# State-space convolution with LoRA tiles on one core: the first eight heads of the kernel K in two halves, warm-up matmuls from the start, D partly added on VectorE, and the eighth pair of x behind strip 2

## The chip, the cores and the metric

The kernel runs on one core of a Trainium2 chip. Its time is the device time of one execution in microseconds (us). TensorE is the matrix engine (PE in the rows), VectorE is DVE, ScalarE is ACT, GpSimd is POOL, and SyncE (SP) only issues transfers here. Sixteen DMA engines serve all queues. PEld is TensorE loading its stationary operand beside its own matmuls.

## The reference

Two stages over x of shape (128, 32, 512): batch, head, position.

```python
# stage 1: a long convolution by head, K computed from the parameters
dtA = (-exp(log_A_real) + 1j * A_imag) * exp(log_dt)[:, None]
K   = 2 * einsum('hn,hnl->hl', Cc * (exp(dtA) - 1) / A, exp(dtA[:, :, None] * arange(512))).real
y   = causal_conv(x, K) + x * D[:, None]          # by FFT in the reference
x   = x + y * (arange(512) < length[b])
# stage 2: a linear layer of 512 x 512 and a LoRA adapter chosen by batch row
x   = x + x @ W.T + bias + (x @ A[id].T) @ B[id].T
```

## The kernel before

**K.** For each of 32 heads the 512 values of K are a 16 x 32 product over the states, so a head is one small matmul (128x16 by 128x32, both real parts stacked). VectorE makes the factors from sines and magnitudes, which ScalarE computes; POOL and VectorE make the small coefficients (`sm`, `rc`, `mm`, `ct`) ahead of that. The heads go in four groups of eight (`GROUPS`, `group` on VectorE and on TensorE). A group's product in PSUM gets D added at lag 0 by one more small matmul (`row0` by `d_sb`, L915). ScalarE rounds the group to the short form (`k_hi`, L479) and copies it (L482), VectorE subtracts to get the remainder (`k_low`, L670), and ScalarE's queue stores both into a padded array in HBM, `k_pad` (L487).

**Convolution.** For each head, SP loads a "strip" from `k_pad`: 128 partitions, each the same 512 pairs shifted by one position, 512 KB (`load_strip`, L263). TensorE multiplies it with x of that head in twelve matmuls (L932, `head`): four lengths (512, 384, 256 and 128 columns), each for high x high, remainder x high and high x remainder. There are six strip buffers, so strip n is issued once head n - 6 is done. Strip 0 comes in two halves of 256 KB. x arrives in pairs of heads of 512 KB (`load_pair`, L240), eight pairs ahead of everything and the others behind certain strips (`X_AT`). The adapter's A and B and the weight w come in halves behind strips too (`A_AT`, `B_AT`, `W_AT`). ScalarE rounds x (L462), VectorE subtracts (L741) and masks each head's result into `z_all` (L747).

**Tiles.** Behind the convolution 32 tiles of 128 rows follow. `first_tile` and `tile_base` (L981 to L989, L971) multiply by w, `tile_h` (L959) by the gathered A, `tile_b` (L997, L998) adds h times the gathered B. B's table is written to HBM and gathered from there by POOL (L417). The x tiles 0 to 3 (`x_t`), the two table stores and the bias are issued on SP behind strips 30 and 31. On VectorE x tile 2 is added (`x1_of`, L792) ahead of h of tile 0 (`h_masked`, `h_remainder`, L811).

**What sets the order.** Every engine runs its list as written; semaphores hold it where the program says. All loads and strips are on SP's one queue, in the order of the code. Until its first strip TensorE runs 15 and 2 warm-up matmuls (`keep_warm`, L904), whose result isn't used.

Of the kernel before, what the change touches and what calls it, by code (L numbers as in the profile page):

```python
# [6 lines left out]
F32 = mybir.dt.float32  # L7
# [48 lines left out]
GROUPS = ((0, 8), (8, 16), (16, 24), (24, 32))  # L56
G = 8
NG = len(GROUPS)
XS = 4
# [21 lines left out]
K_AFTER = {2: 7, 3: 14}  # L81
WARM_0, WARM_1 = 15, 2
# [7 lines left out]
def build(nc, x_conv, x_tile, params, table, d_row, length, ids_all, w_t, bias, a_t, b_rows, out):  # L90
    ctx = ExitStack()
    with ctx:
# [40 lines left out]
        k_hi = sb("k_hi", [NA, G, NC], F32R)  # L133
        k_sb = sb("k_sb", [NA, KS, G, NC, 2])
# [54 lines left out]
        k_stored, pad_stored, strip_begun = sem("k_stored"), sem("pad_stored"), sem("strip_begun")  # L189
# [7 lines left out]
        k_hi_put = sem("k_hi_put")  # L197
# [40 lines left out]
        def _(sp):  # L238
# [17 lines left out]
            for n in range(2, PRE):  # L256
                load_pair(n)

# [10 lines left out]
            for h in range(NH):  # L269
                for k, (h0, h1) in enumerate(GROUPS):  # L270
                    if h == h0:
                        sp.wait_ge(k_stored, 16 * (k + 1))
                if h >= SS:
                    sp.wait_ge(conv_done, h + 1 - SS)
                if h == 0:
                    load_strip(h, 0, 0, L // 2, strip_begun)
                    load_strip(h, 0, L // 2, L, strip_landed[0])
# [49 lines left out]
        def _(pool):  # L327
            steps = [0]

            def link(ins):  # L330
# [6 lines left out]
            g.memset(zero[:, :], 0.0).then_inc(zeroed, 1)  # L337
            link(g.memset(row0[:, :], 0.0))
            g.memset(row0[:, 0:1], 1.0).then_inc(zeroed, 1)
            link(g.memset(eye[:, :], 0.0))  # L340
            g.affine_select(out=eye[:, :], in_=eye[:, :], compare_op=ALU.not_equal, fill=1.0,
                            base=0, pattern=[[-1, P]], channel_multiplier=1).then_inc(eye_ready, 1)
            pool.wait_ge(eye_ready, 1)
# [9 lines left out]
            link(g.tensor_scalar(par[:, 3:5, :], par[:, 3:5, :], tab[:, NL:NL + 1], None, ALU.mult))  # L353
            link(g.tensor_tensor(sm[:, 1, :], ai, ai, ALU.mult))
            link(g.tensor_tensor(sm[:, 6:8, :], par[:, 4:6, :], twice(ai), ALU.mult))
            pool.wait_ge(ea_ready, 1)
            link(g.tensor_tensor(sm[:, 0, :], ea[:, :], ea[:, :], ALU.mult))
            link(g.tensor_tensor(sm[:, 2, :], sm[:, 0, :], sm[:, 1, :], ALU.add))
            link(g.tensor_scalar(rc[:, 0, :], sm[:, 2, :], 0.5, None, ALU.mult))
            link(g.tensor_tensor(sm[:, 4:6, :], par[:, 2:4, :], twice(ea[:, :]), ALU.mult))  # L360
            link(g.tensor_tensor(mm[:, 0, 0, :], sm[:, 4, :], sm[:, 6, :], ALU.subtract))
            link(g.tensor_tensor(mm[:, 0, 1, :], sm[:, 5, :], sm[:, 7, :], ALU.add))
            pool.wait_ge(th_ready, 1)
# [9 lines left out]
            link(g.tensor_tensor(mm[:, 1, 1, :], sm[:, 6, :], sm[:, 4, :], ALU.subtract))  # L373
            link(g.tensor_tensor(mm[:, 1, 0, :], sm[:, 5, :], sm[:, 7, :], ALU.add))
# [3 lines left out]
            pool.wait_ge(factors, 2)  # L378

            g.iota(pos, pattern=[[P, LC], [0, NB]], base=0, channel_multiplier=1).then_inc(pos_ready, 1)  # L380
# [70 lines left out]
        def _(act):  # L451
# [12 lines left out]
            def group_sines(k):  # L464

                n = GROUPS[k][1] - GROUPS[k][0]
                act.wait_ge(reduced, k + 1)
                act.activation(sines[:, 0:n, :], xx[:, 0:n, :], ACT.Sin, scale=TURN).then_inc(sines_ready, 1)

            def group_store(k):  # L470

                (h0, h1), s = GROUPS[k], k % KS
                n = h1 - h0
                act.wait_ge(k_done, k + 1)
                if k >= KS:
                    act.wait_ge(k_stored, 16 * (k + 1 - KS))
                if k >= 1:
                    act.wait_ge(k_lo_done, k)
                act.activation(k_hi[:, 0:n, :], k_ps[0:NA, s, 0:n * NC].rearrange("a (h c) -> a h c", c=NC),  # L479
                               ACT.Copy).then_inc(k_hi_done, 1)  # L480
                act.wait_ge(k_hi_done, k + 1)
                act.activation(k_sb[:, s, 0:n, :, 0], k_hi[:, 0:n, :].bitcast(F32), ACT.Copy).then_inc(k_hi_put, 1)  # L482
                act.wait_ge(k_hi_put, k + 1)
                act.wait_ge(k_lo_done, k + 1)
                if k >= 1:
                    act.wait_ge(k_stored, 16 * k)
                act.dma_start(k_pad[h0:h1, P:PAD, :].rearrange("h (a c) e -> a h (c e)", a=NA),  # L487
                              k_sb[:, s, 0:n, :, :].rearrange("a h c e -> a h (c e)")
                              ).then_inc(k_stored, 16)
# [6 lines left out]
            act.activation(ea[:, :], par[:, 0, :], ACT.Exp).then_inc(ea_ready, 1)  # L496
            act.wait_ge(zr_ready, 1)
            act.activation(th[:, :], zr[:, :], ACT.Tanh, scale=0.5).then_inc(th_ready, 1)
            act.wait_ge(table_in, 16)
# [18 lines left out]
            magnitudes(18, 24)
            split_x(3)
            for h in range(XS, NH):  # L520
# [89 lines left out]
        def _(dve):  # L610
# [54 lines left out]

            def k_low(k):

                n, s = GROUPS[k][1] - GROUPS[k][0], k % KS
                dve.wait_ge(k_hi_done, k + 1)
                V.tensor_tensor(k_sb[:, s, 0:n, :, 1], k_ps[0:NA, s, 0:n * NC].rearrange("a (h c) -> a h c", c=NC),  # L670
                                k_hi[:, 0:n, :].bitcast(F32), ALU.subtract).then_inc(k_lo_done, 1)

            def group(k):

                (h0, h1), s = GROUPS[k], k % KS
# [4 lines left out]
                def wide(a, m):  # L680
                    return a[:, h0:h1].unsqueeze(2).to_broadcast((P, n, m))

                def turns():
                    link(V.tensor_tensor(u[:, :, NA:NA + NL], wide(turn, NL), lag, ALU.mult))
# [14 lines left out]

                def multiply():  # L700

                    dve.wait_ge(sines_ready, k + 1)
# [3 lines left out]
                    link(V.tensor_tensor(g2[:, 0:n, :, :], sines[:, 0:n, 0:2 * NA].rearrange("p h (o a) -> p h o a", o=2),  # L706
                                         both, ALU.mult))
                    link(V.tensor_tensor(gg[:, s, 0:n, :], g2[:, 0:n, 0, :], g2[:, 0:n, 1, :], ALU.add))

                def scale():  # L710
                    dve.wait_ge(mags, h1)
                    V.tensor_tensor(gg[:, s, 0:n, :], gg[:, s, 0:n, :], mag[:, h0:h1, 0:NA], ALU.mult).then_inc(factors, 1)
                    V.tensor_tensor(ee[:, s, 0:n, :], sines[:, 0:n, 2 * NA:NA + NL], mag[:, h0:h1, NA:NL],
                                    ALU.mult).then_inc(factors, 1)

                return [turns, phases, whole, fraction, multiply, scale]
# [34 lines left out]
            turns, phases, whole, fraction, multiply, scale = group(0)  # L751
# [7 lines left out]
            multiply()  # L759
            scale()  # L760
            turns, phases, whole, fraction, multiply, scale = group(1)
            turns()
            phases()
            whole()
            k_low(0)
            fraction()
            remainder(0)
# [3 lines left out]
            k_low(1)  # L771
# [4 lines left out]
            beside = {h: do for k, at in STEPS_AT.items() for h, do in zip(at, group(k))}  # L776
            for h in range(XS, NH):
                head(h - XS)
                for k, last in K_AFTER.items():
                    if h == last + XS:  # L780
                        k_low(k)
# [117 lines left out]
        def _(pe):  # L899

            def keep_warm(n):

                for _ in range(n):
                    nc.tensor.matmul(y_ps[:, 0, :], xp[:, 0, 0, 0, :], xp[:, 0, :, 0, :], start=True, stop=True)  # L904

            def group(k):
# [5 lines left out]
                for i in range(h1 - h0):  # L912
                    nc.tensor.matmul(k_ps[0:NA, s, i * NC:(i + 1) * NC], gg[:, s, i, :], ee[:, s, i, :],  # L913
                                     start=(i == 0), stop=False)
# [3 lines left out]
            def head(h):  # L918

                if h == 0:  # L920
                    pe.wait_ge(strip_begun, 16)
# [6 lines left out]
                for n, (m, t, e) in enumerate(terms):  # L928

                    if h == 0 and (m, t, e) == (LC // 2, 0, 0):  # L930
                        pe.wait_ge(strip_landed[0], 16)
# [157 lines left out]
```

## Time and profile before

| | us |
|---|---|
| median of 3 runs | 210.45 (210.29 to 210.97) |
| profiled execution | 210.57 |
| its span | 208.5 |

| engine | busy us | share of the span |
|---|---|---|
| TensorE matmul | 190.8 | 91% |
| VectorE | 168.1 | 81% |
| ScalarE | 120.9 | 58% |
| POOL | 90.3 | 43% |

The span runs from the first to the last instruction on the device. A busy share is an average over stages with different limits, so it is the stages that are read: K and preload to about 21 us, convolution to about 86 us, tiles from there. Matmuls are pipelined and the length of one in a row is longer than its step from the one before.

### The profile page before, as it was taken

The page shows a single profiled execution, that of the slowest core. Times are in us where ns is not written, and L with a number is a line of the kernel's source. Part 1 is how long each engine was busy: PE and PEld are TensorE (multiplying, and loading weights), DVE is VectorE, ACT ScalarE, POOL GpSimd, SP SyncE. Part 2 cuts the span into 40 slices and gives each one's busy share as a digit, 9 for nine tenths or more (in the row PEclk, how much of TensorE's full clock was granted, in tenths as well). Part 3 has the DMA queues.
Part 4 walks back from the last instruction along what each step waited for, and adds up shares of the span by engine and source line. Part 5 has one row for each costly group of instructions (what it writes and reads, how often), then busy time and mean ns, then how long its engine had stood idle before and what let it go on. Part 6 is the DMA issues. An engine that isn't in the chain of part 4 may idle for free.

```text
span 208.5 us, 4394 instructions
## 1 busy us (share of the span) xinstructions
PE 190.8 (91%) x1063; PEld 166.4 (80%) x1063; DVE 168.1 (81%) x368; ACT 120.9 (58%) x354; POOL 90.3 (43%) x144
## 2 busy tenths in 40 slices
PE   0049999999999999899999999999999999999994
PEld 0037999999999899787888888888888888888883
DVE  3985598789799976877999978788888878888662
ACT  2798974343736446237767656657566565656530
POOL 4850000001356778085564645546455464545500
PEclk9999999999999999999999999999999999999999
DMA  5973999999999999983767666677776676765324
GB/s 141 400 310 105 377 410 409 409 413 406 412 411 407 409 407 422 339 262 105 257 238 247 217 207 228 214 201 224 213 222 204 216 229 201 218 200 186 103 101 151
DMA packets 21520, 56.46 MB, mean 271 GB/s; under 512 B 3266, under 2 KB 3970, under 8 KB 21250
## 3 DMA queue, kind: packets, MB, share of 16 engines
q1 hardware_dynamic: 18002, 47.55, 62.2%
q0 software_dynamic: 2560, 8.39, 13.3%
q10 hardware_dynamic: 944, 0.36, 0.7%
q8 instruction: 5, 0.08, 0.2%
q14 instruction: 9, 0.07, 0.1%
HBM read 45.64 MB, written 10.65 MB: 270 GB/s over the span
## 4 chain that ended last, share of the span: by engine, by line
PE 87%; DMA 6%; DVE 4%; POOL 1%; issue 1%; DVEq 0%
PE z_ps L932 26%; PE y_ps L971 20%; PE k_ps L971 20%; PE z_ps L959 7%; DMA strip<-k_pad 5%; PE y_ps L904 3%; PE y_ps L998 2%; PE y_ps L997 2%; PE k_ps L998 2%; PE k_ps L997 2%; PE k_ps L913 1%; DMA par<-params 1%; PE y_ps L1020 1%; PE k_ps L1020 1%; PE y_ps L981 1%
## 5 line engine op out<-in xcount | busy, mean ns | idle before, releaser
L932 PE MATMUL z_ps<-xp,strip 128*128 128x512 f32 (+3 forms) x384 | 63.4, 326 | 0.3 <-DMA strip<-k_pad 0.3
L932 PEld LDWEIGHTS z_ps<-xp,strip 128*128 128x128 f32 x384 | 59.3, 196 | 4.3 <-DMA strip<-k_pad 0.4
L417 POOL DMA_INDIRECT b_hl<-b_tab,b_idx x32 | 37.7, 1178 | 15.3 <-issue 8.5
L412 POOL CAST ag<-a_hl 128x128 fp32r x64 | 23.3, 367 | 41.0 <-PE z_ps L959 30.4
L971 PE MATMUL y_ps<-w_hi,xp 128*128 128x512 f32 x120 | 39.5, 390 | 0.0
L971 PE MATMUL k_ps<-w_hi,xp 128*128 128x512 f32 x120 | 39.5, 390 | 0.0
L550 ACT ACTIVATE ag<-a_hl 128x64 fp32r x128 | 25.6, 249 | 20.5 <-issue 20.3
L462 ACT ACTIVATE xp<-z_all 128x512 fp32r<-128x512 f32 x32 | 19.7, 627 | 19.7 <-PE z_ps L932 18.2
L741 DVE TENSOR_TENSOR xp<-z_all,xp 128x512 fp32r<-128x512 f32 x32 | 26.5, 827 | 5.3 <-ACT xp L462 5.2
L971 PEld LDWEIGHTS y_ps<-w_hi,xp 128*128 128x128 f32 x120 | 22.5, 188 | 4.3
L971 PEld LDWEIGHTS k_ps<-w_hi,xp 128*128 128x128 f32 x120 | 22.5, 188 | 4.2
L747 DVE TENSOR_TENSOR z_all<-z_ps,mask 128x512 f32<-128x512 f32 (+2 forms) x33 | 22.1, 669 | 4.2 <-PE z_ps L932 3.9
L570 ACT ACTIVATE h_hi<-h_m 64x128 fp32r<-64x128 f32 x64 | 19.5, 305 | 9.1 <-DVE h_m L806 7.0
L971 PE MATMUL y_ps<-w_lo,xp 128*128 128x512 f32 x60 | 23.4, 390 | 0.0
L971 PE MATMUL k_ps<-w_lo,xp 128*128 128x512 f32 x60 | 23.4, 390 | 0.0
L399 POOL TENSOR_TENSOR a_hl<-a_raw,a_hl 128x512 fp32r<-128x512 f32 x4 | 6.0, 1512 | 38.5 <-ACT a_hl L540 38.5
L558 ACT ACTIVATE xp<-x_t 128x512 fp32r<-128x512 f32 x30 | 19.0, 632 | 5.5 <-DVE x_t L792 4.8
L959 PEld LDWEIGHTS z_ps<-xp,ag 128*128 128x128 f32 x128 | 19.3, 188 | 3.4 <-issue 0.5
L792 DVE TENSOR_TENSOR x_t<-x_t,z_all 128x512 f32<-128x512 f32 x30 | 20.5, 684 | 0.6 <-DMA x_t<-x_tile 0.6
L796 DVE TENSOR_TENSOR xp<-x_t,xp 128x512 fp32r<-128x512 f32 x30 | 20.3, 677 | 0.7 <-ACT xp L558 0.7
L959 PE MATMUL z_ps<-xp,ag 128*128 128x256 f32 x128 | 20.2, 281 | 0.1
L563 ACT ACTIVATE h_b<-z_ps 64x256 f32<-64x256 f32 x32 | 12.1, 379 | 12.4 <-PE z_ps L959 12.4
(138 smaller groups left out, 239.4 us busy)
## 6 DMA issues: line engine op xcount, KB each, us to landing
strip<-k_pad SPq DMA_DIRECT2D x31, 512.0 KB, 7.9
z_all<-x_conv SPq DMA_DIRECT2D x16, 512.0 KB, 8.5
x_t<-x_tile SPq DMA_DIRECT2D x32, 256.0 KB, 2.8
out<-a_raw SPq DMA_DIRECT2D x31, 256.0 KB, 2.4
a_raw<-a_t SPq DMA_DIRECT2D x2, 512.0 KB, 8.3
x_t<-b_rows SPq DMA_DIRECT2D x2, 512.0 KB, 8.8
w_sb<-w_t SPq DMA_DIRECT2D x2, 512.0 KB, 10.0
b_tab<-b_hl SPq DMA_DIRECT2D x1, 1024.0 KB, 10.1
```

The lines of the kernel that those rows point to most:

```text
L412: last = g.tensor_copy(ag[:, s, :, :, q, :].rearrange("p c e r -> p e c r"), src)
L417: g.indirect_dma_start(out=b_hl[:, t % BS, :].bitcast(F32), out_offset=None, in_=b_tab, in_offset=bass.IndirectOffsetOnAxis(ap=b_idx[:, t: ...
L462: act.activation(xp[:, h % XS, :, 0, :], z_all[:, h, :, :], ACT.Copy).then_inc(xc_hi_done, 1)
L550: last = act.activation(ag[:, s, :, e, q, :], src[:, e, :, :], ACT.Copy)
L570: act.activation(h_hi[o:o + BR, b, :], h_m[:, b, :], ACT.Copy).then_inc(hhi_done, 1)
L741: V.tensor_tensor(xp[:, h % XS, :, 1, :], z_all[:, h, :, :], xp[:, h % XS, :, 0, :].bitcast(F32), ALU.subtract).then_inc(xc_lo_done, 1)
L747: V.tensor_tensor(z_all[:, h, :, b0:b1], in_chunks(z_ps[:, h % ZS, :])[:, :, b0:b1], mask[:, :, b0:b1], ALU.mult).then_inc(z_masked, 1)
L792: V.tensor_tensor(xt, xt, z_rows(t), ALU.add).then_inc(x1_done, 1)
L796: V.tensor_tensor(xp[:, s % XS, :, 1, :], in_chunks(x_t[:, s % XT, :]), xp[:, s % XS, :, 0, :].bitcast(F32), ALU.subtract).then_inc(xlo_do ...
L932: last = nc.tensor.matmul(z_ps[:, h % ZS, m * P:L], strip[:, h % SS, m * P:(m + 1) * P, t], xp[:, h % XS, 0:LC - m, e, :], start=(n == 0), ...
L959: last = nc.tensor.matmul(h_ps[:, s % TS, 0:2 * P], ag[:, s % TS, c, :, :, :].rearrange("p e b r -> p (e b r)"), xp[:, s % XS, c, :, :].re ...
L971: last = nc.tensor.matmul(y_bank(s), xp[:, s % XS, c, e, :], w[:, c, :], start=(n == 0), stop=False)
```

## The change

1. **K's first eight heads in two groups of four.** `GROUPS` now has 4, 4, 8, 8, 8 heads; sines and phases stay in sets of eight (`SETS`). TensorE forms the third product (heads 8 to 15) before head 0.
2. **Rounding in one step.** ScalarE rounds straight into `k_sb`; `k_hi` and its copy are gone.
3. **Stores.** Groups 0, 1 and 2 are stored from SP's queue (`store_k`), groups 3 and 4 from ScalarE's as before. There is a semaphore for each of the two `k_sb` buffers.
4. **Warm-ups.** TensorE runs 12 warm-ups on a buffer of ones from the start, then 5, 4, 4 and 5 behind the angles, the shifted angles, the small sines and the first set's sines, and 10, 3 and 5 behind the second product.
5. **Strip 1 in halves**, as strip 0.
6. **D.** For groups 3 and 4 VectorE adds D at lag 0 in PSUM (`k_first_lag`) in place of the matmul, and ScalarE's rounding waits for it.
7. **Coefficients.** The factor 2 moves into the table and into two ScalarE scalings; POOL forms all four `mm` terms before it waits for the reciprocal; `eye` is filled later.
8. **Transfers.** Seven pairs of x ahead of the strips, the eighth behind strip 2. Pair 15 goes from behind strip 24 to behind 25, w's second half from behind 26 to behind 27.

```diff
-GROUPS = ((0, 8), (8, 16), (16, 24), (24, 32))
+SETS = ((0, 8), (8, 16), (16, 24), (24, 32))
+GROUPS = ((0, 4), (4, 8), (8, 16), (16, 24), (24, 32))
+BY_SP = 3
-X_AT = {7: 8, 10: 9, 13: 10, 15: 11, 18: 12, 20: 13, 22: 14, 24: 15}
+X_AT = {2: 7, 7: 8, 10: 9, 13: 10, 15: 11, 18: 12, 20: 13, 22: 14, 25: 15}
-A_AT, B_AT, W_AT = {9: 0, 12: 1}, {17: 0, 19: 1}, {24: 0, 26: 1}
+A_AT, B_AT, W_AT = {9: 0, 12: 1}, {17: 0, 19: 1}, {24: 0, 27: 1}
-K_AFTER = {2: 7, 3: 14}
-WARM_0, WARM_1 = 15, 2
+K_AFTER = {3: 7, 4: 14}
+WARM = (12, 5, 4, 4, 5)
+WARM_K = (10, 3, 5)
...
+        def store_k(engine, k):
+            (h0, h1), s = GROUPS[k], k % KS
+            engine.dma_start(k_pad[h0:h1, P:PAD, :].rearrange("h (a c) e -> a h (c e)", a=NA),
+                             k_sb[:, s, 0:h1 - h0, :, :].rearrange("a h c e -> a h (c e)").bitcast(F32)
+                             ).then_inc(k_stored[s], 16)
...
-            for n in range(2, PRE):
+            for n in range(2, PRE - 1):
                 load_pair(n)
+            for k in range(KS):
+                sp.wait_ge(k_lo_done, k + 1)
+                store_k(sp, k)
...
-                        sp.wait_ge(k_stored, 16 * (k + 1))
+                        sp.wait_ge(k_stored[k % KS], 16 * (k // KS + 1))
+                if h == SS:
+                    sp.wait_ge(k_lo_done, BY_SP)
+                    store_k(sp, BY_SP - 1)
...
+            def rounded_rows(k):
+                n, s = GROUPS[k][1] - GROUPS[k][0], k % KS
+                act.wait_ge(k_done, k + 1)
+                if k in K_AFTER:
+                    act.wait_ge(d_added, 1 + list(K_AFTER).index(k))
+                if k >= KS:
+                    act.wait_ge(k_stored[s], 16 * (k // KS))
+                act.activation(k_sb[:, s, 0:n, :, 0], ..., ACT.Copy).then_inc(k_hi_done, 1)
...
+            magnitudes(8, 11)
+            rounded_rows(0)
+            magnitudes(11, 13)
+            rounded_rows(1)
+            magnitudes(13, 16)
+            set_sines(1)
...
+            pe.wait_ge(warm_ready, 1)
+            keep_warm(WARM[0])
+            for n, (ready, count) in enumerate(((turn_ready, 1), (angle_ready, 1), (cs_ready, 1), (sines_ready, 1))):
+                pe.wait_ge(ready, count)
+                keep_warm(WARM[1 + n])
             pe.wait_ge(d_in, 16)
             pe.wait_ge(zeroed, 2)
             group(0)
-            pe.wait_ge(xc_hi_done, 1)
-            keep_warm(WARM_0)
             group(1)
-            keep_warm(WARM_1)
+            keep_warm(WARM_K[0])
+            pe.wait_ge(reduced, 2)
+            keep_warm(WARM_K[1])
+            pe.wait_ge(sines_ready, 2)
+            keep_warm(WARM_K[2]).then_inc(warmed, 1)
+            group(KS)
```

SP's list from the preload to the strips of the second eight heads, before (`z_all<-x_conv` is a pair of x, `x5` five in a row):

```order
L240 DMA z_all<-x_conv 128x1024 x6
L263 DMA strip<-k_pad 128x512 [waits k_stored,pad_stored]
L263 DMA strip<-k_pad 128x512
L263 DMA strip<-k_pad 128x1024 x5
L283 DMA ids<-ids_all 128x160
L263 DMA strip<-k_pad 128x1024 [waits conv_done] x2
L240 DMA z_all<-x_conv 128x1024
L263 DMA strip<-k_pad 128x1024 [waits conv_done,k_stored]
```

and in the changed program:

```order
L250 DMA z_all<-x_conv 128x1024 x5
L230 DMA k_pad<-k_sb 16x4x64 [waits k_lo_done] x2
L277 DMA strip<-k_pad 128x512 [waits k_stored0,pad_stored]
L277 DMA strip<-k_pad 128x512 x3
L277 DMA strip<-k_pad 128x1024
L250 DMA z_all<-x_conv 128x1024
L277 DMA strip<-k_pad 128x1024
L277 DMA strip<-k_pad 128x1024 [waits k_stored1]
L277 DMA strip<-k_pad 128x1024
L300 DMA ids<-ids_all 128x160
L230 DMA k_pad<-k_sb 16x8x64 [waits k_lo_done]
L277 DMA strip<-k_pad 128x1024 [waits conv_done] x2
```

One pair has moved from ahead of the stores to behind strip 2, and three stores stand in this queue now, the third between ids and strip 6.

ScalarE's list around the first rounding, before:

```order
L462 ACTIVATE xp<-z_all 128x4x128 [waits x_landed0]
L504 ACT_TABLE_LOAD
L504 ACTIVATE mag<-tab,zr 128x48 x8
L479 ACTIVATE k_hi<-k_ps 16x256 [waits k_done]
L482 ACTIVATE k_sb<-k_hi 16x256 [waits k_hi_done]
L487 DMA k_pad<-k_sb 16x8x64 [waits k_lo_done,k_hi_put]
```

and after:

```order
L482 ACTIVATE xp<-z_all 128x4x128 [waits x_landed0]
L522 ACT_TABLE_LOAD
L522 ACTIVATE mag<-tab,zr 128x48 x3
L498 ACTIVATE k_sb<-k_ps 16x128 [waits k_done]
L522 ACTIVATE mag<-tab,zr 128x48 x2
L498 ACTIVATE k_sb<-k_ps 16x128 [waits k_done]
L522 ACTIVATE mag<-tab,zr 128x48 x3
```

The first rounding stands behind three magnitudes and no longer behind eight, and neither the copy nor the store is in this list.

## Rows read from the trace of the kernel before

**Rows 1.** The page's 40 slices of 5.2 us: TensorE's busy tenths and GB/s

```profile
PE   0049999999999999899999999999999999999994
...
GB/s 141 400 310 105 377 410 409 409 413 406 412 411 407 409 407 422 339 262 105 257 238 247 217 207 228 214 201 224 213 222 204 216 229 201 218 200 186 103 101 151
```

**Rows 2.** Windows: length, busy us by engine (instructions), granted clock, DMA share, GB/s

```profile
13.40:21.35 7.95, 7.92 (x53) 6.26 (x54) 5.25 (x13) 6.74 (x16) 2.21 (x5) 1.00 0.42 138
21.35:37.00 15.65, 15.65 (x97) 14.68 (x95) 13.17 (x26) 10.50 (x26) 0.00 (x0) 1.00 1.03 400
...
62.30:72.40 10.10, 9.80 (x61) 9.07 (x60) 10.10 (x14) 5.48 (x10) 7.07 (x7) 1.00 1.03 410
...
86.50:208.50 122.00, 118.24 (x590) 99.82 (x590) 98.60 (x230) 71.41 (x246) 59.14 (x92) 1.00 0.64 203
```

**Rows 3.** Timeline of TensorE: start us, us, line, operation, count, idle before

```profile
52.29 19.79 PE L932 MATMUL z_ps<-xp,strip 128*128 128x512 f32 x120
72.38 13.91 PE L932 MATMUL z_ps<-xp,strip 128*128 128x512 f32 x84 [0.30 <-DMA strip<-k_pad]
87.07 1.16 PE L981 MATMUL y_ps<-w_hi,xp 128*128 128x512 f32 x4 [0.78 <-DVE xp L870]
...
93.63 0.39 PE L997 MATMUL y_ps<-b_hl,h_hi 128*128 128x512 f32 x1
```

**Rows 4.** Timeline of VectorE at the first tiles

```profile
89.09 0.69 DVE L792 TENSOR_TENSOR x_t<-x_t,z_all 128x512 f32<-128x512 f32 x1 [0.57 <-DMA x_t<-x_tile]
...
92.86 0.53 DVE L811 TENSOR_TENSOR h_lo<-h_m,h_hi 64x128 fp32r<-64x128 f32 x1
```

**Rows 5.** Timeline of SP's issues (strips 0 to 6; 21, 22; 25, 26; tile 2 on)

```profile
17.42 3.38 SPq L263 DMA_DIRECT2D strip<-k_pad  x7
...
54.47 2.28 SPq L263 DMA_DIRECT2D strip<-k_pad  x2
...
62.31 2.29 SPq L263 DMA_DIRECT2D strip<-k_pad  x2
...
76.83 14.71 SPq L266 DMA_DIRECT2D x_t<-x_tile  x5
```

**Rows 6.** Issue to landing: pair 7 (5.7), strips 0a (17.4), 21, 25, tile 2

```profile
DMA to landing us min/median/max: 9.7/9.7/9.7
...
DMA to landing us min/median/max: 3.0/3.0/3.0
...
DMA to landing us min/median/max: 8.9/8.9/8.9
...
DMA to landing us min/median/max: 10.0/10.0/10.0
...
DMA to landing us min/median/max: 12.1/12.1/12.1
```

**Rows 7.** Timeline of all engines around the first group of K

```profile
9.68 0.26 ACT L508 ACTIVATE cs<-cs_x 128x64 f32<-128x64 f32 x1
...
10.25 0.63 ACT L468 ACTIVATE work<-work 128x512 f32<-128x512 f32 x1 [0.31 <-DVE work L698]
...
11.29 0.29 DVE L662 TENSOR_TENSOR cs_m<-cs,mm 128x128 f32<-128x128 f32 x1 [0.60 <-POOL mm L376]
...
12.71 1.91 ACT L504 ACTIVATE mag<-tab,zr 128x48 f32<-128x48 f32 x8
...
14.64 0.37 ACT L479 ACTIVATE k_hi<-k_ps 16x256 fp32r<-16x256 f32 x1
...
15.14 0.41 DVE L670 TENSOR_TENSOR k_sb<-k_ps,k_hi 16x256 f32<-16x256 f32 x1
...
15.65 0.33 ACTq L487 DMA_DIRECT2D k_pad<-k_sb  x1
```

**Rows 8.** Timeline of TensorE before head 0

```profile
14.53 5.63 PE L904 MATMUL y_ps<-xp 128*128 128x512 f32 x15
20.09 0.64 PE L913 MATMUL k_ps<-ee,gg 128*16 128x32 f32 x16
```

More of the change, by code:

```diff
@@ L188, in build @@
         tab_hi_stored, tab_lo_stored = sem("tab_hi_stored"), sem("tab_lo_stored")
-        k_stored, pad_stored, strip_begun = sem("k_stored"), sem("pad_stored"), sem("strip_begun")
+        k_stored = [sem(f"k_stored{s}") for s in range(KS)]
+        pad_stored, strip_begun = sem("pad_stored"), [sem(f"strip_begun{n}") for n in range(2)]
         pool_step, dve_step = sem("pool_step"), sem("dve_step")
@@ L337, in _ @@
             g.memset(zero[:, :], 0.0).then_inc(zeroed, 1)
+            pool.wait_ge(zeroed, 1)
+            g.memset(xp[:, XS - 1, :, 0, :].bitcast(F32), 1.0).then_inc(warm_ready, 1)
+            pool.wait_ge(warm_ready, 1)
             link(g.memset(row0[:, :], 0.0))
             g.memset(row0[:, 0:1], 1.0).then_inc(zeroed, 1)
[L340 to L343, printed above, removed]
+            pool.wait_ge(zeroed, 2)
             ai = par[:, 1, :]
@@ L377, in _ @@
             pool.wait_ge(scaled, 1)
-            pool.wait_ge(factors, 2)
+            pool.wait_ge(factors, 2 * KS)
+            link(g.memset(eye[:, :], 0.0))
+            g.affine_select(out=eye[:, :], in_=eye[:, :], compare_op=ALU.not_equal, fill=1.0,
+                            base=0, pattern=[[-1, P]], channel_multiplier=1).then_inc(eye_ready, 1)
+            pool.wait_ge(eye_ready, 1)
             g.iota(pos, pattern=[[P, LC], [0, NB]], base=0, channel_multiplier=1).then_inc(pos_ready, 1)
@@ L750, in _ @@
             small_angles()
-            turns, phases, whole, fraction, multiply, scale = group(0)
+            turns, phases, whole, fraction = set_of(0)
             turns()
@@ L758, in _ @@
             coefficients()
-            multiply()
-            scale()
-            turns, phases, whole, fraction, multiply, scale = group(1)
+            for k in range(KS):
+                multiply, scale = group(k)
+                multiply()
+                scale()
+            turns, phases, whole, fraction = set_of(1)
+            k_low(0)
             turns()
+            k_low(1)
             phases()
             whole()
-            k_low(0)
             fraction()
+            multiply, scale = group(KS)
             remainder(0)
@@ L770, in _ @@
             remainder(1)
-            k_low(1)
+            k_low(KS)
             masks()
@@ L774, in _ @@
             remainder(3)
-            beside = {h: do for k, at in STEPS_AT.items() for h, do in zip(at, group(k))}
+            beside = {h: do for k, at in STEPS_AT.items() for h, do in zip(at, set_of(k) + group(k + 1))}
             for h in range(XS, NH):
@@ L903, in keep_warm @@
                 for _ in range(n):
-                    nc.tensor.matmul(y_ps[:, 0, :], xp[:, 0, 0, 0, :], xp[:, 0, :, 0, :], start=True, stop=True)
+                    last = nc.tensor.matmul(y_ps[:, 0, :], xp[:, XS - 1, 0, 0, :], xp[:, XS - 1, :, 0, :],
+                                            start=True, stop=True)
+                return last
             def group(k):
@@ L912, in group @@
                 for i in range(h1 - h0):
-                    nc.tensor.matmul(k_ps[0:NA, s, i * NC:(i + 1) * NC], gg[:, s, i, :], ee[:, s, i, :],
-                                     start=(i == 0), stop=False)
+                    last = nc.tensor.matmul(k_ps[0:NA, s, i * NC:(i + 1) * NC], gg[:, s, i, :], ee[:, s, i, :],
+                                            start=(i == 0), stop=(k in K_AFTER and i == h1 - h0 - 1))
+                if k in K_AFTER:
+                    last.then_inc(k_done, 1)
+                    return
                 nc.tensor.matmul(k_ps[0:NA, s, 0:(h1 - h0) * NC:NC], row0[:, :], d_sb[:, h0:h1],
@@ L1062 @@
     table[:, 0:NL] = np.concatenate([NC * np.arange(NA), np.arange(NC)])
-    table[:, NL] = np.repeat((1.0, -1.0), NS)
+    table[:, NL] = np.repeat((2.0, -2.0), NS)
     table[:, NL + 1] = np.repeat((-0.25, 0.0), NS)
```

110 lines of the change are left out of this document (54 added, 56 removed).

## The prediction

> **What bounds the kernel now.** I read the slices first, then the windows by stage, then the timelines of TensorE and VectorE at the joints, and last the landing time of single transfers. The slices show TensorE busy from the fourth slice to the end and the DMA engines near 400 GB/s from 20.8 to 88 us [rows 1]. The stage table says which of the two has room: from 21.35 us the sixteen DMA engines have a busy share of 1.03 at 400 to 410 GB/s while TensorE is busy for all but 0.3 us; from 86.5 us on TensorE is as busy, but DMA has a share of 0.64 [rows 2]. So two resources are full at once in the convolution, one in the tiles. Which is the tighter shows in three places. Strip 25 landed after TensorE was free for it: a 0.30 us wait at 72.38 [rows 3]. VectorE waited 0.57 us for x tile 2, which started it at 89.09 [rows 4]; that tile was issued at 76.83 and landed 12.1 us later, at 88.9 [rows 5, 6]. And behind it hangs the first tile: VectorE adds tile 2 before it masks h of tile 0, and h_lo of tile 0 was done at 92.86 + 0.53 = 93.39; TensorE took it at 93.63, 0.24 us later, with no idle time in front [rows 3, 4]. In short: the head of the tile stage is set by TensorE and by the DMA queue within 0.24 us of each other. Everything between the first strip's issue at 17.42 and x tile 2 lands in queue order, each 512 KB about 1.28 us behind the one before (0.524 MB at 410 GB/s [rows 2]), because the queue never runs dry.
>
> That gives the rule of this forecast: the tile stage can start earlier only by as much as BOTH TensorE's start and the DMA queue move.
>
> **TensorE's side.** K is now made in products of 4, 4, 8, 8, 8 heads. Before head 0 stand the two halves, and then the third product too, which was the second before. The second eight heads' factors were taken at 20.09, though TensorE had been running its 15 warm-ups until then [rows 8]. After: VectorE spends an estimated 0.7 us more on two half groups than on one whole, but starts 0.6 us sooner (below), and ScalarE reaches the second sine an estimated 0.5 us sooner, since its copy of the rounded rows and its wait for the remainder are gone. I put the third product between 19.0 and 20.1, head 0 behind it (0.64 us and an estimated 0.2 for D's) between 19.8 and 20.9, against 21.35, where stage 1 of the table ends. TensorE's own lead is then 0.45 to 1.55 us. Taking D's small product out of groups 3 and 4 gives under 0.1 us each (their eight heads take 0.64 [rows 8]), hidden by the strips; the added 1x8 addition on VectorE and ScalarE's wait for it (an estimate of 0.2 to 0.7 us at heads 11 and 18) lie beside convolution heads of 1.98 us (120 matmuls, so ten heads, in 19.79 [rows 3]) with three split heads in hand. Cost nothing; without that cover 0.7 us each.
>
> **DMA's side, first term: the strips start earlier.** Before: first rounding at 14.64, remainder at 15.14, store issued 15.65, strip 0 issued 17.42, so 1.77 us from store to strips [rows 5, 7]. After:
> - The coefficients: POOL has its two mm steps behind and the halving folded into the table, so the 0.60 us that VectorE waited for POOL at 11.29 [rows 7] goes. Four heads instead of eight take off an estimated 0.35. The first product, done before the warm-ups' 14.53 [rows 8], now begins at 12.5 and is over by 13.0, if the warm-ups ahead of it are (rival 2).
> - But what then ends last is ScalarE: its magnitudes start at 12.71, eight in 1.91 us [rows 7], 0.24 each, and three stand ahead of the first rounding: 12.71 + 0.72 = 13.43. So most of the coefficient gain is not used; the rounding moves by 14.64 - 13.43 = 1.21 us.
> - Half as many elements: the rounding took 0.37 and the remainder 0.41 for 16x256. For 16x128 I take 0.30 and 0.28 (bounds: half and all). With the same gap of 0.13 between them and 0.10 to the issue: 13.43 + 0.30 + 0.13 + 0.28 + 0.10 = 14.24, against 15.65: 1.41 us earlier (1.2 to 1.6).
> - The store moves from ScalarE's queue to SP's, behind seven x pairs. Its 1.77 us I keep. The nearest other transfer, the first strip half, took 3.0 us to land [rows 6]; so the shift could be 0.2 at worst, and at best 1.8 if half the rows save 0.2.
> First strips at 16.0: **1.41 us earlier**.
>
> **DMA's side, second term: x pair 7.** It leaves the preload, behind which the engines had time to spare (138 GB/s over 13.40 to 21.35 [rows 2]), and enters the full stage behind strip 2. It is 512 KB: **1.28 us later** for everything behind it until x tile 2. Nothing in the full stage gives that back. What does the move buy? Pair 7 landed at 5.7 + 9.7 = 15.4 [rows 6], and the first store now lands about 15.9.
> The Trainium skill (DMA: Bandwidth & Descriptors, section Queues, rings and completion order) says that a DMA's semaphore increment lands only after every earlier write of that engine, across its queues. By that rule a store behind eight pairs could not be reported before 15.4, and behind seven not before about 14.1; both lie ahead of 15.9, so by the rule the move buys nothing at the first strip, and by the rows neither, since the store is issued at 14.2, where seven pairs have landed. This trace agrees as far as it can: the store before was issued behind pair 7's landing and SP passed it 1.77 us later.
>
> Pair 15 moves from strip 24 to 25 and w's second half from 26 to 27: for x tile 2 they change nothing; strips 25 and 27 come 1.28 us sooner against their neighbours, 26 and 28 do not.
>
> **The sum.** DMA: -1.41 + 1.28 = -0.13 us at x tile 2. TensorE: at least -0.45 at head 0. Along the way the strips hold it back: strip 21 landed at 54.47 + 8.9 = 63.4 and its head began at 52.29 + 6 x 1.98 = 64.2, so 0.8 + 0.13 of lead is all that fits; strip 26 (the second issue of the row at 62.31, 1.28 us behind strip 25's 72.3) lands at 73.5 for a head that began at 74.36: 0.9. The convolution ends up to 0.9 us sooner, VectorE then waits for x tile 2 up to 1.3 us where it waited 0.57, TensorE waits for h_lo of tile 0, and the tiles start 0.13 us sooner. The tiles themselves are the same code. Against the profiled execution, 210.57 (span 208.5 and 2.1 around it): 210.4. The median shown is 210.45, 0.1 below the profiled one: **210.3**.
>
> **Rivals.**
> 1. The lead reaches the tiles (faster). If x tile 2 comes with the lead, because the early slow stretch of the queue shrinks (from 13.40 to 21.35 it moved 138 GB/s, and pair 7 could fill holes in it), TensorE's limit counts: -0.9, so 209.6. For it: only 0.3 us idle of TensorE before, and strips landing 3.0 us after issue show a slow start that isn't bytes. Against: one queue, in order, full at 410 GB/s. 26%.
> 2. The warm-ups delay the first product (slower). A convolution head (3,840 columns in 1.98 us) gives at most 0.26 us for 512 columns; the fifteen warm-ups took 5.63 us [rows 8], not 3.9, so most ran at the 1.2 GHz level, 0.43 us each, though the granted clock of that stretch reads 1.00 [rows 2]. After: four hang on the cosines (9.68 + 0.26 = 9.94) and five on the sines (10.25 + 0.63 = 10.88) [rows 7]. At the 2.4 GHz level they end at 12.2, before the factors. At 1.2 GHz they end at 9.94 + 9 x 0.43 = 13.8; the product of half the heads takes up to its old 1.0, rounding starts at 14.8 instead of 13.43, the strips move by about -0.1 instead of -1.4, and the sum is +1.2: 211.6. It decides where TensorE is slow again at 10 us, after twelve warm-ups from about 1.6 us and an idle stretch of an estimated 1.1 us behind them. Before shows 0.78 us of idling ahead of 87.07 [rows 3] with four matmuls in 1.16 behind it, the fast level. 9%.
> 3. The third store on SP's queue (slower). It is issued behind strips 3 to 5 and ids, so it lands with them near 29 us, and strip 8 waits for it, SP standing still; strips 6, 7 and pair 8 (3.8 us) are in the queue meanwhile. Strip 8 need only be issued by about 31; if it isn't, each us later is one lost. About +1: 211.3. 4%. The first store landing 3.0 us after issue in place of 1.77 gives +1.1 as well, another 4%.
>
> **How the numbers follow.** Forecast 57%, its own range 209.8 to 211.0 (the shift from 0.8 to 1.8 us against 1.28, and 0.15 of spread). Rival 1 26%, slower ones 17%. What this kernel's measurement can tell from no change is 0.3%, 0.63 us. Of the forecast's share 3 points fall faster and 3 slower. Faster 0.28, same 0.53, slower 0.19. Range 209.4 to 211.3: below it lies a lead of over 1.05 us, above it most of rival 2.
>
> **What would show it.** First K store issued on SP at 14.2, first strip at 16.0; head 0 between 19.8 and 20.9; more DMA waits of TensorE around heads 20 to 26; VectorE waiting about 1.3 us for x tile 2; that tile landing at 88.8, not 88. It is wrong if x tile 2 lands at 88.2 or sooner, if the first strip is issued after 16.8, or if the wait at x tile 2 doesn't reach TensorE.

## The result and the profile after

| | before | after |
|---|---|---|
| median of the runs | 210.45 us (5 runs, 210.29 to 210.97) | 211.9 us (5 runs, 211.55 to 212.51) |
| profiled execution, span | 210.57, 208.5 | 211.55, 209.8 |

The ratio, with its 95% interval, is 1.0057 [1.0043, 1.0071]: slower by 1.2 us. The forecast was 210.3, in 209.4 to 211.3, and held "the same" for likeliest and "slower" for least likely. Run again with the third group of experiments below, the changed kernel gave 1.0023 [1.0003, 1.0043]: slower again; the two intervals just meet at 1.0043, so the cost lies between some 0.5 and 1.2 us. The forecast was wrong, in sign and in size.

The prologue first, which answers to [rows 7, 8]. This is the timeline of all engines of the changed kernel; columns are start, length, engine, line, operation, tiles, count, and the idle time before it with what ended it.

```profile
9.20 3.26 PE L949 MATMUL y_ps<-xp 128*128 128x512 f32 x13 [0.18 <-POOL cs_x L388]
...
12.65 0.39 PE L960 MATMUL k_ps<-ee,gg 128*16 128x32 f32 x8 [0.18 <-DVE ee L752]
...
12.75 0.79 ACT L522 ACTIVATE mag<-tab,zr 128x48 f32<-128x48 f32 x3
...
13.56 0.28 ACT L498 ACTIVATE k_sb<-k_ps 16x128 fp32r<-16x128 f32 x1
...
13.87 0.28 DVE L700 TENSOR_TENSOR k_sb<-k_ps,k_sb 16x128 fp32r<-16x128 f32 x1 [0.44 <-ACT k_sb L498]
...
14.17 1.10 SPq L230 DMA_DIRECT2D k_pad<-k_sb  x2
...
15.71 2.24 SPq L277 DMA_DIRECT2D strip<-k_pad  x5
```

The first product is over by 13.04, so ScalarE's three magnitudes end last (12.75 + 0.79 = 13.54), the store goes out at 14.17 and the first strip at 15.71, where it was 17.42 [rows 5]. The thirteen warm-ups take 3.26 us, with a step of 0.23 us from one to the next; the first nine of the twelve from the start of the program have a step of 0.43. The granted clock reads 1.00 for both.

TensorE's side, answering to [rows 3, 8]; the timeline of TensorE of the changed kernel:

```profile
19.16 0.64 PE L960 MATMUL k_ps<-ee,gg 128*16 128x32 f32 x16 [0.17 <-DVE ee L752]
...
19.86 4.06 PE L982 MATMUL z_ps<-xp,strip 128*128 128x512 f32 x24
24.16 2.17 PE L982 MATMUL z_ps<-xp,strip 128*128 128x512 f32 x12 [0.24 <-DMA strip<-k_pad]
...
86.80 1.16 PE L1039 MATMUL y_ps<-w_hi,xp 128*128 128x512 f32 x4 [0.71 <-DVE xp L915]
...
95.07 0.47 PE L1055 MATMUL y_ps<-b_hl,h_hi 128*128 128x512 f32 x1 [1.57 <-DVE h_lo L856]
```

Head 0 begins at 19.86, 1.49 us sooner than 21.35. At the end of the convolution only 0.27 is left of that (86.80 against 87.07), and at the first h of the tiles TensorE stands still for 1.57 us where it had no idle time: 95.07 against 93.63. What it waits for hangs on VectorE, which answers to [rows 4]; the timeline of VectorE:

```profile
90.65 0.69 DVE L837 TENSOR_TENSOR x_t<-x_t,z_all 128x512 f32<-128x512 f32 x1 [2.33 <-DMA x_t<-x_tile]
...
94.40 0.52 DVE L856 TENSOR_TENSOR h_lo<-h_m,h_hi 64x128 fp32r<-64x128 f32 x1
```

VectorE waits 2.33 us for x tile 2, where it waited 0.57, and starts 1.56 later. So the gate is the one the prediction named, the DMA queue at x tile 2, and the queue is late there: 90.6 where 88.8 was forecast. The span grew by 1.3 us. The windows, answering to [rows 2] (length, busy us by engine, clock, DMA share, GB/s):

```profile
13.40:21.35 7.95, 7.37 (x54) 5.58 (x55) 6.65 (x16) 7.13 (x18) 4.35 (x7) 1.00 0.55 175
21.35:37.00 15.65, 15.12 (x106) 13.96 (x105) 13.86 (x28) 9.43 (x23) 0.00 (x0) 1.00 1.02 372
...
62.30:72.40 10.10, 9.84 (x61) 9.15 (x60) 10.10 (x14) 4.94 (x9) 7.24 (x7) 1.00 1.03 410
86.50:208.50 122.00, 118.33 (x590) 99.81 (x590) 98.27 (x229) 71.72 (x246) 60.10 (x92) 1.00 0.66 204
```

The early stage moved more (175 GB/s against 138), and the stage from 21.35 to 37 moved less: 372 against 400, at nearly the same busy share. In 15.65 us that is 0.44 MB, 1.07 us of the full rate. The place shows in a finer cut of it, the changed kernel's windows of seven and three us:

```profile
30.00:37.00 7.00, 7.00 (x59) 6.58 (x57) 6.31 (x14) 3.22 (x5) 0.00 (x0) 1.00 1.02 364
...
34.00:37.00 3.00, 3.00 (x34) 2.81 (x33) 2.97 (x8) 0.63 (x1) 0.00 (x0) 1.00 1.00 309
```

and the same seven us of the kernel before:

```profile
30.00:37.00 7.00, 7.00 (x46) 6.62 (x44) 6.28 (x14) 3.59 (x6) 0.00 (x0) 1.00 1.03 411
```

What SP did differently ahead of that stretch, in its timeline of the changed kernel, with the time from issue to landing of the third K store and of strip 8:

```profile
20.83 0.49 SPq L230 DMA_DIRECT2D k_pad<-k_sb  x1
...
29.58 0.80 SPq L277 DMA_DIRECT2D strip<-k_pad  x2
```

```profile
DMA to landing us min/median/max: 8.7/8.7/8.7
...
DMA to landing us min/median/max: 4.9/4.9/4.9
```

and its waits (what it waited for, us in total, times, longest):

```profile
SPq L277 <- DMA k_pad<-k_sb: 5.1, 2, 3.2
```

The store was issued at 20.83 behind strips and landed at 29.5; SP stood still 3.2 us for it, and strip 8 went out at 29.58, where before it went out at 27.53. In both kernels the store's landing releases strip 8: before, it landed at 27.5. Strip 8 itself wasn't late: it landed at 34.5, before at 27.53 + 7.6 = 35.1. It is what follows that came slowly. Pair 8, just ahead of strip 8, landed at 33.2 (before 33.9), so 0.7 us to the good; the first half of A, two transfers behind strip 8, at 38.0 (before 37.7), so 0.3 to the bad. One us was lost between the two.

### The profile page after: what moved, and what is told of

Its sections match the earlier page's. It is cut to its first block, busy times and chain, and to the rows that moved or that the text cites. A ratio compares the mean times of both kernels' runs of the same rounds, so it can differ in the third digit from the quotient of the medians.

```text
span 209.8 us, 4461 instructions
## 1 busy us (share of the span) xinstructions
PE 199.5 (95%) x1092; PEld 171.6 (82%) x1092; DVE 169.4 (81%) x375; ACT 119.9 (57%) x353; POOL 93.0 (44%) x143
## 4 chain that ended last, share of the span: by engine, by line
PE 77%; DMA 11%; DVE 6%; ACT 2%; issue 2%; SPq 1%; ACTq 0%; DVEq 0%
PE z_ps L982 23%; PE k_ps L1029 20%; PE y_ps L1029 18%; DMA strip<-k_pad 9%; PE z_ps L1017 7%; PE y_ps L1055 2%; PE y_ps L1056 2%; PE k_ps L1056 2%; PE k_ps L1055 2%; DMA par<-params 1%; SPq L277 1%; DMA k_pad<-k_sb 1%; PE y_ps L1078 1%; PE k_ps L1078 1%; ACT L522 1%
## 5 line engine op out<-in xcount | busy, mean ns | idle before, releaser
L982 PE MATMUL z_ps<-xp,strip 128*128 128x512 f32 (+3 forms) x384 | 64.2, 326 | 1.0 <-DMA strip<-k_pad 1.0
L432 POOL CAST ag<-a_hl 128x128 fp32r x64 | 24.2, 383 | 40.3 <-PE z_ps L1017 27.5
L573 ACT ACTIVATE ag<-a_hl 128x64 fp32r x128 | 25.6, 248 | 19.8 <-issue 19.6
L482 ACT ACTIVATE xp<-z_all 128x512 fp32r<-128x512 f32 x32 | 19.8, 626 | 21.1 <-PE z_ps L982 19.1
```

The lines of the kernel that those rows point to most:

```text
L432: last = g.tensor_copy(ag[:, s, :, :, q, :].rearrange("p c e r -> p e c r"), src)
L482: act.activation(xp[:, h % XS, :, 0, :], z_all[:, h, :, :], ACT.Copy).then_inc(xc_hi_done, 1)
L573: last = act.activation(ag[:, s, :, e, q, :], src[:, e, :, :], ACT.Copy)
L982: last = nc.tensor.matmul(z_ps[:, h % ZS, m * P:L], strip[:, h % SS, m * P:(m + 1) * P, t], xp[:, h % XS, 0:LC - m, e, :], start=(n == 0), ...
```

## The experiments

Three theories. Late issue (L): strip 8, issued late because it waits for the third K store in SP's queue, costs 1 to 1.5 us of transfer time. The pair: pair 7 behind strip 2 costs its 1.28, as forecast, and what the early strips bring is lost in another way. The halves: the halves of strips 0 and 1, or the stores themselves, make slow transfers. The expectations call late issue L or S; Q is that a transfer costs the queue its bytes and nothing else; R is that the store standing in SP's queue (its ring) makes the slow stretch.

**First group: one part undone at a time** (the kernel before on that chip 210.77). Each ratio is to the kernel before. The changed kernel wasn't run in this group, so a difference from it is one of two ratios that were taken apart; its own two ratios, 1.0057 and 1.0023, show that this is sure to some 0.7 us only.

Pair 7 back in the preload:

```diff
-X_AT = {2: 7, 7: 8,
+X_AT = {7: 8,
-for n in range(2, PRE - 1): load_pair(n)
+for n in range(2, PRE): load_pair(n)
```

> The changed kernel with pair 7 back in the preload (eight pairs ahead of the stores). Theory Q, the queue's length decides: x tile 2 is added 1.28 us sooner than at 90.65, so at about 89.4, first strip still issued near 15.7 to 15.9; time about 210.6. Theory S, slow stretches and the late strip 8 decide and not the pair: x tile 2 near 90.3, time 211.5 or more.

Measured 210.66, ratio 0.9991 [0.9962, 1.0021]; span 208.7, x tile 2 waited for until 89.50. Against the changed kernel that is 1.1 us less in span, and the first h of the tiles moved with x tile 2, from 95.07 to 93.92. Pair 7's price is near the forecast. Its window has the slow stretch too, and larger, with strip 8 issued at 28.53:

```profile
30.00:37.00 7.00, 7.00 (x55) 6.45 (x55) 6.28 (x14) 2.42 (x4) 0.00 (x0) 1.00 1.02 328
```

Pair 7 between the first and the second K store:

```diff
-X_AT = {2: 7, 7: 8,
+X_AT = {7: 8,
 ...
                 store_k(sp, k)
+                if k == 0:
+                    load_pair(PRE - 1)
```

> The changed kernel with pair 7 issued between the first and the second K store. Theory Q: the pair moves while the engines have nothing else, the second store waits for it and lands near 17.5, still ahead of strip 4; as with the pair in the preload about 210.6. If the first store or strip 0 is held back by the pair, the first strip comes up to 1.3 us later and nothing is gained: 211.9.

Measured 211.11, ratio 1.0000 [0.9978, 1.0022]; span 209.4. The second store, issued at 15.27, landed at 18.8 behind the pair, and TensorE waited 0.43 us for strip 0's second half at 22.01. Its time lies between that of the changed kernel and that of the run above, within the interval of the latter: no gain by this place.

The third K store on ScalarE's queue, all else as changed:

```diff
-                if h == SS:
-                    sp.wait_ge(k_lo_done, BY_SP)
-                    store_k(sp, BY_SP - 1)
 ...
             magnitudes(17, 19)
+            act.wait_ge(k_lo_done, BY_SP)
+            store_k(act, BY_SP - 1)
```

> The changed kernel with the third K store (heads 8 to 15) on ScalarE's queue as before. Theory S: the store lands 5.6 us after its issue near 20.8, so at 26.5 in place of 29.5, strip 8 is issued near 26.5 in place of 29.58, the slow stretch at 34 to 36.5 us goes and x tile 2 comes 0.9 us sooner: about 211.0. Theory Q: the queue is full without a gap anyway, nothing moves: 211.9.

Measured 210.64, ratio 0.9998 [0.9967, 1.0029], the same as the kernel before, as the forecast had it for the whole change. Its timeline of SP, its window and its timeline of VectorE:

```profile
27.59 1.73 SPq L277 DMA_DIRECT2D strip<-k_pad  x2
```

```profile
30.00:37.00 7.00, 7.00 (x53) 6.58 (x52) 6.32 (x13) 3.42 (x5) 0.00 (x0) 1.00 1.03 410
```

```profile
89.59 0.69 DVE L836 TENSOR_TENSOR x_t<-x_t,z_all 128x512 f32<-128x512 f32 x1 [1.82 <-DMA x_t<-x_tile]
```

Strip 8 goes out where it did in the kernel before, the stretch from 30 to 37 is at full rate, and x tile 2 is 1.06 us sooner than in the changed kernel. The store, issued at 20.81, took 6.8 us to land, and ids, issued ahead of it on SP at 20.0, landed only at 29.6. By this one edit strip 31 lands at 81.84 in place of 82.38.
The Trainium skill (DMA: Bandwidth & Descriptors, section Queues, rings and completion order) says that SP and ScalarE each have a queue row of their own, and that each DMA engine takes turns between the rows that have work. This run agrees: the store on ScalarE's row passed ids on SP's row, while on SP's row it landed with ids (29.5 and 29.3).

The kernel before with the one edit to pair 7:

```diff
-for n in range(2, PRE): load_pair(n)
+for n in range(2, PRE - 1): load_pair(n)
-X_AT = {7: 8,
+X_AT = {2: 7, 7: 8,
```

> The kernel before with only pair 7 moved from the preload to behind strip 2. Theory Q: x tile 2 1.28 us later than at 89.09, the first strip unchanged at 17.4: 210.45 + 1.2 = 211.7. If the pair fills holes in the slow start of the strips: 210.5 to 210.9.

Measured 212.25, ratio 1.0054 [1.0031, 1.0076]: 1.1 us for pair 7 by itself (0.7 to 1.6). In its trace strip 8 lands 1.26 us later than before (36.43 for 35.17) and strip 31 1.39 later, near the forecast of 1.28. X tile 2, at 91.28, is 2.19 later: the rest comes behind strip 31, in a stretch whose length varies (see what stays open).

**Second group** (before 210.93). Both parts undone, pair 7 in the preload and the third store on ScalarE's queue:

> The changed kernel with both: pair 7 in the preload and the third K store on ScalarE's queue. Each alone took 1.24 us off. If they are two separate losses of one queue they add: x tile 2 near 88.2, and 209.5 (then TensorE's side, some 0.9 us behind the kernel before, is as near a bound as the queue). If one hides the other: 210.6 again.

Measured 209.79, ratio 0.9943 [0.9926, 0.9959]: faster than before by 1.2 us. So the early strips do pay, when neither cost stands against them. x tile 2 was waited for until 88.99. The timeline of TensorE shows a new wait in it:

```profile
64.00 2.44 PE L981 MATMUL z_ps<-xp,strip 128*128 128x512 f32 x13 [1.36 <-DVE xp L779]
```

VectorE's block on the adapter ids (L760 to L766, 59.41 to 62.2) stands ahead of the remainder that TensorE waits for.

The same with strip 1 in one piece:

```diff
-                if h < 2:
+                if h < 1:
                     load_strip(h, h, 0, L // 2, strip_begun[h])
 ...
```

and the same limit in TensorE's `head`.

> As e5, with strip 1 in one piece. If the halves (2 KB a partition) are what slows the queue at 20 to 24 us (280 to 350 GB/s there, 350 to 400 in the same place behind the start of the kernel before), x tile 2 comes up to 0.8 us sooner than in e5 and the time is up to 0.5 us shorter. If they aren't: the same within 0.3 us.

Measured 209.68, ratio 0.9946 [0.9928, 0.9964], against 0.9943 for the run above: the same, within some 0.5 us. From 20 to 24 us it moved 363 GB/s and the run above 360. In its one trace x tile 2 comes 0.61 us sooner (88.38), 0.3 of it by pair 8's landing, which the time doesn't show. So nothing shows that the halves cost anything; a few tenths stay possible.

The third store on ScalarE's queue, and strip 8 held until head 4's convolution is done:

```diff
-                    sp.wait_ge(conv_done, h + 1 - SS)
+                    sp.wait_ge(conv_done, 5 if h == 8 else h + 1 - SS)
```

> e3 (third K store on ScalarE's queue) with strip 8 held until head 4 is done, near 30.4 us, in place of 27.6. Theory L, the late issue of strip 8 makes the slow stretch: it comes back near 34 to 37 us though no store is in SP's queue, and the time rises to 211.9 or more. Theory R, the store standing in SP's ring makes it: no slow stretch, 210.6 to 211.0.

Measured 213.35, ratio 1.0119 [1.0100, 1.0138]. SP's timeline, the window and VectorE's timeline:

```profile
31.07 0.80 SPq L277 DMA_DIRECT2D strip<-k_pad  x2
```

```profile
30.00:37.00 7.00, 7.00 (x51) 6.58 (x51) 6.31 (x13) 3.48 (x5) 0.00 (x0) 1.00 0.98 304
```

```profile
91.75 0.69 DVE L836 TENSOR_TENSOR x_t<-x_t,z_all 128x512 f32<-128x512 f32 x1 [1.70 <-DMA x_t<-x_tile]
```

The third store isn't in SP's queue here, and the slow stretch is back and deeper. Strip 8 landed 3.9 us after its issue, at 35.0, against 34.7 in the run without the hold: again hardly late itself. So SP's standing still makes a loss with no store in its way. The hold stops all of SP, so what stands behind strip 8 goes out later too; the runs don't part strip 8 from that.

Both parts undone, and x tile 2 issued ahead of the two table stores:

```diff
             load_x_tile(1, 1)
+            load_x_tile(2, 2)
             store_table(0, b_hl
 ...
-            load_x_tile(2, 2)
             load_x_tile(3, 3)
```

> As e5, with x tile 2 issued ahead of the two table stores in place of behind the bias. If x tile 2 is the gate of the tiles, VectorE's wait of 1.3 to 2.3 us for it goes, and the tiles start with TensorE: 0.3 to 0.8 us below e5, unless the gathered rows of B (table landed 0.64 us later) end last then. If the gate is elsewhere: as e5.

Measured 209.34, ratio 0.9929 [0.9912, 0.9946]. This is the fastest version, ahead of both kernels; from the one without the tile's edit (0.9943) its interval doesn't part it. TensorE, which stood still 0.23 us at h of tile 0 without the edit, no longer does:

```profile
92.06 0.50 PE L1054 MATMUL y_ps<-b_hl,h_hi 128*128 128x512 f32 x1
```

**Third group** (before 210.96). The third store on ScalarE's queue, and strip 8 held until head 3 is done (4 in place of the 5 above):

> The changed kernel with the third K store on ScalarE's queue, and strip 8 held until the convolution of head 3 is done (in place of head 2), which puts its issue near 29.4 us, about where the changed kernel has it, with nothing else of the changed kernel's order back. Late-issue theory (strip 8 issued two us late is the whole loss): ratio to the kernel before 1.004 to 1.009, slow transfers again somewhere between 30 and 37 us, x tile 2 waited for 1.0 to 1.5 us later than in the run with the store alone moved (89.6 us). Store theory (the store's own descriptors in the strips' ring cost it, the issue time does not): ratio 0.997 to 1.002, no slow stretch.

Measured 211.32, ratio 1.0021 [1.0001, 1.0042].

```profile
28.87 0.80 SPq L277 DMA_DIRECT2D strip<-k_pad  x2
```

```profile
30.00:37.00 7.00, 7.00 (x58) 6.57 (x57) 6.31 (x14) 3.24 (x5) 0.00 (x0) 1.00 1.03 373
```

The slow stretch is there with 1.3 us of delay already. The ratio is below the band that was expected by late issue (1.004 to 1.009), and the lower half of its interval lies in that of the store theory; x tile 2 came 0.53 us later than without the hold (90.12), half of what was expected. By the window and the landing it speaks for late issue, by the ratio alone it wouldn't decide.

The kernel before, with strip 8 held until head 4 is done (the same 5 in its own line):

> The kernel before with one edit: strip 8 held until the convolution of head 4 is done, some 3.5 us later than its own 27.5 us. Late-issue theory: it costs this kernel too, with none of the change in it; the same hold cost the changed kernel 2.7 us, so 212.5 to 214, ratio 1.008 to 1.015. If the cost hangs on the change's own order (a store in SP's ring, pair 7 behind strip 2): ratio 0.998 to 1.003.

Measured 213.51, ratio 1.0113 [1.0066, 1.0159].

```profile
31.61 0.80 SPq L263 DMA_DIRECT2D strip<-k_pad  x2
```

```profile
30.00:37.00 7.00, 7.00 (x45) 6.61 (x44) 6.27 (x13) 4.01 (x6) 0.00 (x0) 1.00 0.89 289
```

None of the change is in this kernel, and the same hold costs it 2.4 us. The late-issue theory stands without the rest of the change: what costs is how late SP goes on, not where the store stands.

The fastest version with the ids' block at head 12 in place of 20:

> The best version so far (pair 7 in the preload, third K store on ScalarE's queue, x tile 2 issued ahead of the table stores) with VectorE's block on the adapter ids moved from head 20 to head 12. In two earlier runs that block left TensorE 1.36 us short of a remainder near 64 us, in one it did not. If VectorE's lead limits the convolution there, up to 1 us less: 208.3 to 209.3. If the queue bounds the middle anyway: 209.0 to 209.8, with the stall near head 14 or none.

Measured 209.65, ratio 0.9938 [0.9918, 0.9957]: no gain over the 0.9929 without that edit in the second group. The stall moved with the block: TensorE waited 1.42 us for VectorE at 51.95.

The changed kernel again:

> The changed kernel again, word for word, for a comparison on one chip with the two holds. Expected by both theories: ratio to the kernel before 1.004 to 1.007. By the late-issue theory it and the hold until head 3 agree within 0.3%.

Measured 211.64, ratio 1.0023 [1.0003, 1.0043], the same as the hold until head 3 on that chip (1.0021), as late issue has it; but the ratio is below the 1.004 to 1.007 that was expected. It issued strip 8 at 29.71, moved 347 GB/s from 30 to 37, and had x tile 2 at 90.62.

Together, by the issue time of strip 8; the fourth column is the time from its issue to its landing, and lost is 7 us x (410 - GB/s) / 410:

| kernel | strip 8 issued | GB/s, 30 to 37 us | issue to landing, us | lost, us | strip 31 landed | x tile 2 added at |
|---|---|---|---|---|---|---|
| before | 27.53 | 411 | 7.6 | 0 | 81.93 | 89.09 |
| store on ScalarE's queue | 27.59 | 410 | 7.2 | 0 | 81.84 | 89.59 |
| store on ScalarE's queue, held until head 3 | 28.87 | 373 | 5.7 | 0.6 | 82.45 | 90.12 |
| changed | 29.58 | 364 | 4.9 | 0.8 | 82.38 | 90.65 |
| changed, again | 29.71 | 347 | 4.8 | 1.1 | 83.09 | 90.62 |
| store on ScalarE's queue, held until head 4 | 31.07 | 304 | 3.9 | 1.8 | 84.11 | 91.75 |
| before, held until head 4 | 31.61 | 289 | 3.9 | 2.1 | 84.54 | 92.33 |

In the five rows that share one order of pair 7 and strips, x tile 2 moves with the loss: 0.53, 1.06, 1.03 and 2.16 us later than the first of them, for 0.6, 0.8, 1.1 and 1.8 lost. Strip 31 does so too: 0.61, 0.54, 1.25 and 2.27.

The issue time by itself doesn't order all fourteen traces: pair 7 in the preload lost more (328 GB/s) with strip 8 issued at 28.53 than the hold with 28.87. The time from issue to landing does, which says how much work the queue still held:

| issue to landing of strip 8, us | traces | GB/s, 30 to 37 us |
|---|---|---|
| 6.0 to 8.8 | seven: before, before with pair 7 behind strip 2, the store on ScalarE's queue, and the four with both parts undone | 408 to 411 |
| 5.7 | store on ScalarE's queue, held until head 3 | 373 |
| 4.8 to 4.9 | changed, changed again, pair 7 in the preload, pair 7 between the stores | 364, 347, 328, 344 |
| 3.9 | the two holds until head 4 | 304, 289 |

The lowest of the seven is the one with the ids' block at head 12, 6.0 us and this window:

```profile
30.00:37.00 7.00, 6.92 (x54) 6.34 (x54) 6.31 (x13) 2.31 (x4) 0.00 (x0) 1.00 1.03 410
```

So what counts is how much the queue holds when SP goes on, and pair 7 in the preload, which lets the queue run further down by 28.53, is no exception. This order was read from the traces afterwards; only the three holds were set on purpose.

## Why the prediction was wrong

- **K's store and the first strip: right, a bit too careful.** 14.17 and 15.71 for 14.24 and 16.0, so 1.71 us earlier for 1.41. The first strip followed the store by 1.54 us for the 1.77 kept. The run with both costs undone shows that these microseconds reach the end: 1.2 us of gain.
- **Pair 7: right.** 1.28 forecast; 1.1 measured in the kernel before (1.26 at strip 8's landing), and 1.1 in span against the changed kernel.
- **TensorE's side: right.** Head 0 at 19.86 in 19.8 to 20.9. Of the lead of 1.49 us 0.27 was left at the end of the convolution. Waits for strips took 1.0 us where the kernel before had 0.30: two at heads 21 and 26, as forecast, and two at heads 2 and 3, which weren't. The rest of what went, some 0.5 us, isn't traced.
- **The rivals on the warm-ups and the landing of the first store: out.** Thirteen warm-ups took 3.26 us, and the five behind 0.99 us of idling took 1.43, both with the short step of 0.23 us, the 2.4 GHz level by the prediction's own reading; the granted clock reads 1.00.
- **The gate: right.** VectorE waits at x tile 2, and TensorE behind it. In the run with pair 7 in the preload both came 1.15 us sooner together. With both parts undone and tile 2 ahead of the table stores the wait is gone.
- **The failed step: the third K store in SP's queue, rival 3.** The prediction put its landing near 29 (29.5 measured) and saw SP stand still, but said that "Strip 8 need only be issued by about 31", because 3.8 us of other transfers were queued meanwhile. That took the queue as a line in which a late transfer costs nothing until the line is empty, the same premise as in its opening ("because the queue never runs dry"). The queue didn't run dry here either: strip 8 was issued before 31 and landed in time. Yet the runs show that the price begins much sooner: no loss at 27.6, 0.6 us at 28.87, 0.8 to 1.1 at 29.6 to 29.7, 1.8 at 31.07. So the size of this rival, about +1, was near, and its condition was wrong, which is why it had a chance of 4% and no place in the sum. The edit costs 1.2 us by the first ratio (1.0057 - 0.9998, two sets of runs; 1.0 in span) and 0.5 by the second (1.0023 - 0.9998); at strip 31's landing it is 0.5 in one trace of the changed kernel and 1.25 in the other.

With this one term the sum would give -0.13 + 1.2, so 211.5, where the ratio's 1.2 us on 210.45 is 211.7. That is no independent proof, since the 1.2 is itself the difference of two measured ratios. What stands on its own is strip 31 with the store on ScalarE's queue: 0.09 us sooner than before, where the sum said 0.13.

What stays open. First, why a thin queue slows what is in it already. The busy share falls with the rate only in part (1.02, 0.98, 0.89 for 364, 304, 289 GB/s), so engines stand idle for some of it, and for the rest their packets take longer. That some of the sixteen engines run ahead of the others and find nothing more queued would fit the first part; no run shows single engines. Second, the tail. The changed kernel's queue is 0.4 us behind at strip 31 and 1.6 at x tile 2, and the store on ScalarE's queue is 0.1 ahead at strip 31 and 0.5 behind at x tile 2, with the time the same. From strip 31's landing to that of the bias, four transfers behind it in the same order, it took 6.2 to 7.5 us over thirteen traces, 7.5 and 6.7 in the two of the changed kernel alone. So up to 1 us at x tile 2 in a single trace can be the tail's own spread, and what the tail costs wasn't tried by itself.

## What to carry to other kernels

In a stage where the DMA queue is the bound, look at when each transfer is issued, not only at when it must land: here a transfer that landed 3.9 to 5.7 us after its issue was followed by a slow stretch, one that landed 6.0 us or more after it was not. A store whose landing holds the issuing engine should not go at the end of that engine's own full queue; another engine's queue took 1.9 us off its landing and let SP go on 2 us sooner. And a lead won at the start is spent on the tightest resource behind it: count what each moved transfer adds to that one before counting what it hides.

## What the runs showed of the hardware

- Where SP issued strip 8 so late that it landed 3.9 to 5.7 us after its issue, it landed in time, yet the 7 us around it moved 289 to 373 GB/s; where it landed 6.0 to 8.8 us after its issue they moved 408 to 411. TensorE's granted clock was 1.00 throughout.
- The same 256-column K store landed 8.7 us after issue at the end of SP's queue and 6.8 us after on ScalarE's, beside the same strips; the half store, with the pairs landed, took 1.5 us.
- The changed kernel's ratio was 1.0057 [1.0043, 1.0071] in one set of runs and 1.0023 [1.0003, 1.0043] in another. Both are above 1; whether they differ isn't shown.
